# Score banks of an attention kernel taken pair by pair in the order of the exponentials, half sets written in two parts, and a new placing of the side jobs

## The reference, cut to what matters

```python
x = x + attn(layernorm(x))      # softmax(tril(q k / sqrt(8), -1)) v, then @ Wr + br
x = x + ffn(layernorm(x))
# attn
att = einsum('bhqe,bhke->bhqk', q, k) / sqrt(he)
att = softmax(att * tril(ones, k=-1))
# ffn
scores = where(causal, einsum('bqhd,bkhd->bhqk', q, k) * scale, -inf)
x1 = layer_norm(x + (softmax(scores) @ v) @ out_proj_w.T + b)
gates = softmax(x1 @ gate_w.T + gate_b); top_gates, top_idx = top_k(gates, 2)
moe_out = sum(sel_experts(x1) * top_gates)
return layer_norm(x1 + moe_out)
```

## Time and profile before

| | |
|---|---|
| median of 3 runs | 795.78 us (795.67 to 799.67) |
| the profiled execution | 796.04 us, its span 794.3 us |
| PE busy | 651.4 us (82%) |
| ACT busy | 654.6 us (82%) |
| DVE busy | 394.4 us (50%) |
| POOL busy | 321.0 us (40%) |
| exponentials (ACT, L1378) | 576, 596.5 us |
| granted TensorE clock | 0.954 on average |

### The profile page before, as it was taken

One profiled execution on the slowest core, in us unless ns is written; L12 is line 12 of the kernel. 1 busy time (PEld: TensorE's weight loads), 2 busy tenths in 40 slices (PEclk: granted clock), 3 DMA queues, 4 the chain that ended last, 5 costly groups with the idle time before them and its releaser, 6 DMA issues. The chain is left out here.

```text
span 794.3 us, 15432 instructions
## 1 busy us (share of the span) xinstructions
PE 651.4 (82%) x5560; PEld 245.9 (31%) x5560; DVE 394.4 (50%) x1089; ACT 654.6 (82%) x748; POOL 321.0 (40%) x635
## 2 busy tenths in 40 slices
PE   4588997888799889889988888888978888977753
PEld 3233332333233233233322322223322332323421
DVE  5364453346446643376455633465544522545575
ACT  1589899998798789999889999998879989895341
POOL 3252336215633325334643344435633344333244
PEclk9699999999999999999999999999999999999776
DMA  7856457644667414434545533423635243300010
GB/s 181 276 190 209 135 163 242 200 122 161 205 211 242 160 53 126 134 108 129 186 132 160 173 114 119 135 77 125 204 120 176 93 135 111 109 27 14 1 40 28
DMA packets 76993, 109.79 MB, mean 138 GB/s; under 512 B 13784, under 2 KB 28256, under 8 KB 76896
## 3 DMA queue, kind: packets, MB, share of 16 engines
q1 hardware_dynamic: 72944, 107.32, 42.8%
q10 hardware_dynamic: 3952, 1.30, 0.7%
HBM read 60.91 MB, written 47.68 MB: 137 GB/s over the span
## 5 line engine op out<-in xcount | busy, mean ns | idle before, releaser
L1378 ACT ACTIVATE probs<-scores,shift 128x1024 f32<-128x1024 f32 x576 | 596.5, 1125 | 70.0 <-PE scores L1183 64.4
L1454 POOL TENSOR_SCALAR_AFFINE_SELECT probs<-probs 128x256 f32<-128x256 f32 (+1 forms) x448 | 195.7, 453 | 366.1 <-ACT probs L1378 365.5
L1212 PE MATMUL acc<-probs,v 128*9 128x512 f32 (+3 forms) x3072 | 318.9, 503 | 4.1 <-ACT num L1300 4.1
L1183 PE MATMUL scores<-qs,ks 32*128 32x512 f32 (+3 forms) x1536 | 159.1, 428 | 74.9 <-ACT probs L1378 72.9
L1183 PEld LDWEIGHTS scores<-qs,ks 32*128 32x128 f32 x1536 | 72.4, 187 | 272.5 <-ACT probs L1378 208.2
L1212 PEld LDWEIGHTS acc<-probs,v 128*9 128x9 f32 x3072 | 58.9, 100 | 105.2 <-issue 66.7
L1501 DVE TENSOR_TENSOR prod<-side,G 128x512 f32<-128x512 f32 x41 | 28.3, 691 | 84.3 <-PE side L1165 84.2
L1165 PE MATMUL side<-we,x1T 128*128 128x512 f32 x92 | 53.0, 659 | 0.7 <-DVE part L1550 0.7
L1435 POOL TENSOR_TENSOR moe<-psum 128x256 f32<-128x256 f32 x32 | 25.0, 781 | 67.6 <-DVE psum L1501 55.3
L1300 ACT ACTIVATE num<-acc 128x512 f32<-128x512 f32 x64 | 38.6, 603 | 5.7 <-PE acc L1212 5.6
L1410 POOL TENSOR_TENSOR rstd<-rstd,expo 128x4 f32<-128x4 f32 x32 | 33.3, 1041 | 2.7
(11 more groups left out here) (193 smaller groups left out, 605.6 us busy)
## 6 DMA issues: line engine op xcount, KB each, us to landing
ks<-k_dram SPq DMA_DIRECT2D x96, 256.0 KB, 4.2
q_dram<-part SPq DMA_DIRECT2D x64, 256.0 KB, 3.2
qs<-q_dram SPq DMA_DIRECT2D x64, 256.0 KB, 3.7
num_dram<-num SPq DMA_DIRECT2D x60, 256.0 KB, 2.7
k_dram<-part SPq DMA_DIRECT2D x30, 256.0 KB, 3.6
xrow<-in_x SPq DMA_DIRECT2D x16, 256.0 KB, 4.5
nat<-num_dram SPq DMA_DIRECT2D x15, 256.0 KB
rdenb<-rden_dram SPq DMA_DIRECT2D x15, 256.0 KB
```

Of the source, the lines that this page charges most:

```text
L1183: ins = pe.matmul(scores[:, pair(g, h // 2), h % 2, col:col + w], ks[u][r, kt // TH, (kt % TH) * P:(kt % TH + 1) * P], qs[u][r, q0:q0 + w] ...
L1212: ins = pe.matmul(acc[h * VW:h * VW + VC, q0:q0 + w], v9[V_OF[k]][:, kt, :, HG * hg + h], src, start=(s == 0), stop=last, skip_group_check ...
L1378: act.activation(dst, src, ACT.Exp, bias=shift[:, column(k):column(k) + 1], scale=SCALE).then_inc(probs_raw, 1)
L1454: ins = pool.affine_select(out=blocks, in_=blocks, compare_op=ALU.is_ge, fill=0.0, base=a - 1, pattern=[[0, blocks.shape[1]], [1, P]], cha ...
```

## The change

1. **Pairs by exponential.** Unit `n` (the n-th exponential) has pair `n % 3`. A half set takes one pair: heads 0 and 1 in columns 0 to 255 of its two banks, heads 2 and 3 in columns 256 to 511 of the same banks. PE waits for the exponential three units before the set's last one. Behind a half set that is the exponential before the half set's own.
2. **A half set in two parts.** Since heads 0 and 2 (1 and 3) now share a bank, PE writes heads 0 and 1, then does the values of the set three earlier, then waits for its own first part (`half_scores`) and writes heads 2 and 3; only this tells ACT that the scores are there.
3. **The planner.** `ahead` is measured against the time at which ACT is through with what it has, less the next set's scores; `LATE` goes from 0.5 to 0.2, `UNIT_TIME` from 1.15 to 1.1; the plan's PE and ACT clocks follow points 1 and 2. The due times of `p3`'s stores move later by 50 units and more, so that `p2` stands before `p3`.
4. Slots become `STRETCHES` that could be cut in halves. They aren't here: there is one for each slot, with both halves, and `rows_half` gives the same rows as before.

The diff, cut to its core:

```diff
-def pair(g, i):
-    return (2 * g + i) % PAIRS
...
-    ends[x("store")] = at(k + 2, 40 * j)
+    ends[x("store")] = last_by(k, b, j) + 50
...
-UNIT_TIME = 1.15
-LATE = 0.5
+UNIT_TIME = 1.1
+LATE = 0.2
...
-            ahead = t + (0.49 * len(UNITS_OF[g - LAG]) if p % 2 == 0 and g >= LAG else 0.0) - exps[FIRST_UNIT[g]] - 0.1
+            ahead = t + (values(g) if p % 2 == 0 else 0.0) + next_scores(g) + 0.08 - clock["ACT"]
...
-        def half_block(g, h):
-
-            return h if pair(g, 0) < pair(g, 1) else (h + 2) % HG
+        def place_of(g, h):
+
+            units = UNITS_OF[g]
+            if len(units) == 1:
+                return units[0], h % 2, HALF // 2 * (h // 2)
+            return units[h // 2], h % 2, 0
...
-                else:
-
-                    pe.wait_ge(probs_raw, FIRST_UNIT[g - 1] + 1)
...
+                elif last >= PAIRS:
+
+                    pe.wait_ge(probs_raw, last - PAIRS + 1)
+                if is_half(qh, s):
+                    heads_scores(g, (0, 1), shifted).then_inc(half_scores, 1)
                 else:
...
+                    heads_scores(g, range(HG), shifted).then_inc(scores_ready, 1)
+
+            def other_heads(g, shifted):
+
+                pe.wait_ge(half_scores, HALVES_TO[g])
+                heads_scores(g, (2, 3), shifted).then_inc(scores_ready, 1)
...
                     if g >= LAG:
                         value_group(g - LAG)
+                    if len(UNITS_OF[g]) == 1:
+                        other_heads(g, shifted)
...
-                if len(UNITS_OF[g]) == 1:
-                    low_, high = sorted((pair(g, 0), pair(g, 1)))
-                    src = scores[:, low_:high + 1:high - low_, :, 0:HALF // 2]
-                    dst = probs[n % NPB][:, :, :].rearrange("p a (c s) -> p a c s", c=2)
...
+                src = scores[:, n % PAIRS, :, :].rearrange("p c s -> p (c s)")
+                dst = probs[n % NPB][:, :, :].rearrange("p c s -> p (c s)")
```

More of the change, by code:

```diff
@@ L1 @@
+import itertools
 from contextlib import ExitStack
@@ L36 @@
 NSLOT = len(SLOTS)
+STRETCHES = [(k, (0, 1)) for k in range(NSLOT)]
 def sets_of(qh):
@@ L149, in takes, with stretch_of, pass_of, rows_half @@
     return sum(turn_time(x)[1:])
+def stretch_of(k, qh):
+    return next(st for st, (k_, halves) in enumerate(STRETCHES) if k_ == k and qh in halves)
+def pass_of(k, i):
+    return next(gp for gp in range(NP) if PASS_OF[gp][1] == k and (PASS_OF[gp][2], PASS_OF[gp][3]) == PASSES[i])
+def rows_half(b, j):
+    order = [(SLOTS[k][1], qh) for k, halves in STRETCHES if SLOTS[k][0] for qh in halves]
+    return order[2 * b + j]
+BOUNDS = [(b, 0) for b in range(B)]
+def bound_of(k, _halves):
+    return BOUNDS.index((SLOTS[k][1], 0))
 def at(slot, unit):
-    return slot * UB + unit
+    return (STRETCH_FIRST[stretch_of(slot, 0)] if slot < NSLOT else NU + (slot - NSLOT) * UB) + unit
 def slot_of(a, b):
@@ L238, in p2 @@
         out[x("v")] = [x("xT")]
-        ends[x("parts_out")] = ends[x("v")] = at(k, -12)
+        ends[x("parts_out")] = ends[x("v")] = STRETCH_FIRST[stretch_of(k, j)] - 12
         if j:
[L241 to L245, removed]
+            n = 0
+            out[("p2", b, "top", n)] = [x("norm"), x("norm", 1)]
+            out[("p2", b, "tops", n)] = [("p2", b, "top", n)]
+            out[("p2", b, "roots", n)] = [("p2", b, "tops", n)]
+            out[("p2", b, "shift", n)] = [("p2", b, "roots", n)]
+            ends[("p2", b, "shift", n)] = STRETCH_FIRST[stretch_of(k, 0)] - 4
     def p3(b, j):
@@ L395, in finish, with exponentials, values, next_scores @@
         done[x] = begin + dve + 0.1
+    def exponentials(units):
+        for n in units:
+            clock["ACT"] = max(clock["ACT"], clock["PE"] + 0.08) + 1.0
+            exps[n] = clock["ACT"] + 0.12
+            for gp in range(NP):
+                if evacuated(gp) == n:
+                    clock["ACT"] += 0.48
+                    done[("evacuated", gp)] = clock["ACT"] + 1.5
+    def values(g):
+        return 0.49 * len(UNITS_OF[g - LAG]) if g >= LAG else 0.0
+    def next_scores(g):
+        if g + 1 == SETS_ALL:
+            return 0.0
+        return 0.44 if len(UNITS_OF[g + 1]) > 1 else 0.3 + values(g + 1)
     for p in range(NPOINT):
@@ L1250, in _, with stretch @@
             pe.wait_ge(narrowed, n_narrow)
-            def slot(k, shifted):
-                for g in range(k * GB, (k + 1) * GB):
+            def stretch(st, shifted):
+                for g in range(STRETCH_GROUP[st], STRETCH_GROUP[st + 1]):
                     scores_set(g, shifted)
```

356 lines of the change are left out of this document (196 added, 160 removed).

## The result

The changed kernel takes **804.43 us** (median of 20 runs, 798.97 to 811.78), the kernel before, run beside it on the same chip, 798.61 (20 runs, 795.23 to 804.33): a ratio of **1.0069, 95% interval 1.0046 to 1.0092**. The forecast was 758, faster by 5%. The profiled execution of the changed kernel took 798.97, with a span of 797.2 and a mean granted clock of 0.949 (before: 794.3 and 0.954). That is the fastest of its runs: the three at 0.949 took 798.97 to 801.16, the seventeen others, at 0.929 to 0.945, longer.

The account below looks back on a forecast made before the run. PE and ACT were taken to hold each other up in turn, neither full. Stretch -31 (-38 + 4 + 3 + 0) and tail -7 took 796.04 to 758 us; forecast 744 to 770, wider range 742 to 781.

Parts of the forecast that it names:

- Part 1, first half: Exponentials opening a pass: without a job behind the half set the hole closes; 29 with one keep 0.35 us each.
- Part 1, the gain of 38: 63 pass openings: holes cost 48 us today, 10 stay, so 38 us are gained (22 to 48).
- Part 2: Half sets' scores in two parts: 0.2 us more PE work each, 13 us over 64, costing +4 us (0 to 20).
- a third of it: Share of the split's 13 us of PE work that is paid, only where PE is the later engine.
- no hole: Half sets' own exponentials: scores come about 0.3 us later when PE waits for ACT, leaving ACT without a hole.
- second part comes late: Rival at half sets: exponential delayed behind values and second part, 64 x 1.05 = 67 us, 808 in total; chance 0.07.
- Part 3, +3 and 0 (-10 to +15): Planner: six more jobs before the tail cost +3 us (0 to 7); other holes in the stretch change by 0.
- The tail, -7 (0 to -12): After the last exponential: 7 of 23.6 us between `acc`'s last copy and the last half's sum are saved.
- -31: Stretch from first to last exponential: -38 + 4 + 3 + 0, from 693.1 to 662 us.

Follow-up runs that it names:

- run 1: Against the kernel before: new banks and two-part half sets with the old job table, 1.0056; old banks with the new job table, 1.0072.
- Run 3: The kernel before with only its half sets' scores split in two, the second part waiting for the first: 822.55 us, 1.0271.
- run 2: Changed kernel with the half set's second part directly behind the first, ahead of the values: 0.9971 to the kernel before; with the old job table 1.0052.
- run 5: Kernel before and changed kernel, each with values matmuls cut to three quarters of their columns: 0.9959 and 0.9947 to the kernel before.

## Why the prediction was wrong, point by point

**Part 1, first half: right.** "With no job in between, the hole closes": 34 such openings hold 0.0 us. With a job behind the half set 0.35 each was forecast, and 29 of them hold 6.3, 0.22 each. The holes before openings fell to 6.3 us, where "about 10" was forecast.

**Part 1, the gain of 38: the step that failed.** The sum of the holes was read rightly, their evenness not: of the 63, only some 30 hold about 0.7 us and more with nothing in them, and 22 hold 0.20 to 0.22, where ACT copies `acc` in the gap. What failed is how they were priced. It took 41.0 us of idle at openings as time that the change frees. A hole that closes is a gain only if the next thing that ACT needs is there in time. Of the 63 openings 42 had a job ahead, and at 27 of these PE was late by its own work and waited for no exponential (26.0 of the 41.0 us); 15.0 us at the 36 others stood behind the bank's exponential. The earlier trace rows were read as PE's own hole, and still counted as gain wherever the new order put the job elsewhere. The job's 1 us of PE is not gone by that: it meets the half set instead. PE idled 98 of 693 us before and 87 of 703 after. Openings lost 34.7 us of holes, half sets took back 38.4 (4.3 to 42.7), and the other places gained 6.6; the sum, +10.3, is what the stretch grew by.

**Part 2: the work was sized right; "a third of it" paid and "no hole" failed.** I took 0.2 us of PE for the extra group, 13 us over 64. At full clock the second part takes 0.31 us where a job follows (390.44 to 390.75 above). Where the next scores follow without a wait, they start 0.01 us behind it, on the two strips that it leaves free, and both together take 0.11 us more than the scores alone (0.55 us in 12 such places, as from 411.71 to 412.26, against 0.44, as from 414.31 to 414.75). 29 x 0.31 + 35 x 0.11 is 13 us; with the old table's 42 jobs it is 15, and PE's busy time rose by 15.9 there (run 1). The 25.1 us by which the busy time of these groups rose count the time that they share with the next scores. So the argument that the next scores can start under the second part held, and 0.114 us was its price; that the columns alone set the time did not hold where a job follows.

What failed is what comes of it. Run 3 puts a split that waits for its first part at some 22 us, most of its 28 us of PE paid; how much of the 13 us is paid in the changed kernel no run separates, since the second part's place goes with it. And "half sets' scores are there 0.3 us later: no hole" holds only for the 42 half sets without a job ahead, 0.24 us each; of the 22 with one, 21 held about 1.1 each and one 9.4. The place behind the values was priced at nothing but this; with the new table it costs 1.0% (run 2).

The rule cited there (TensorEngine Tiling (Array Packing), Key Properties, of the Trainium skill) tells of drains at a change of mode. The trace fits it as far as it goes: 0.11 us where scores follow scores, 0.31 us where another kind of matmul follows. That a drain is the reason for the difference, no run here shows.

**The rival "second part comes late": its mechanism is what happened.** It gave 1.05 us for each late half set, and ones with a job ahead cost that. But it put all 64 at that price (67 us, 808 in total), and only the third with a job ahead paid it. That 804 lies near its 808 is luck: it also counted 48 us won, where the openings gave 34.7. I gave it 0.07, on the ground that PE waited at half sets before. That wait was PE's slack under the old banks; with the new banks it is down to 0.3 us. That the parts and the six jobs more are what spent it is argued, not shown.

**Part 3, +3 and 0 (-10 to +15).** The new table alone costs the stretch 11.4 us with the old banks, inside the bounds and far from the centre. One late input makes 9.4 of the holes of the kernel after. The prediction had such inputs as its upper end, in chains through POOL and DMA; the large one ran through DVE's stop at a slot's opening, which it had not seen.

**The tail, -7 (0 to -12): right,** -7.5, and in each kernel with a new table -6.4 to -8.6. The place was half right. From `acc`'s last copy to the last half's sum it is now 17.4 us and not 23.6, but the copy itself comes 2.2 us later behind the last exponential; so the sum begins 21.2 us after the last exponential, 25.2 before. The other 3.5 us were won behind the sum, which the prediction had not counted:

```profile
734.49 0.60 ACT L1398 ACTIVATE num<-acc 128x512 f32<-128x512 f32 x1 [3.82 <-PE scores L1170]
...
751.85 0.68 DVE L1596 TENSOR_TENSOR xrow<-scores,xr 128x512 f32<-128x512 f32 x1
```

**Sum.** Forecast -31 and -7; measured in the profiled executions +10.4 and -7.5, which is 2.9, and a further 3 in the medians. Its median run has a lower clock than its profiled one (0.941 against 0.949); why the clock fell, no run tells by itself.

## What to carry to other kernels

When two engines hold each other up in turn, sort the idle time before a given step by whether its releaser was waiting itself. Only that part belongs to the wait that a change removes; the other is the releaser's own work, and it comes out again at the next step that needs it. A group of side-by-side matmuls that is split has no single price: here the second half cost 0.31 us of PE, as much as the whole group, ahead of other work, 0.11 ahead of matmuls that could start beside it, and 0.44 where it had to wait for the first half. And a signal that a waiting engine needs belongs ahead of the work that it doesn't need. A change of structure should be timed with a plan made from its own traced durations: here the same structure was worth -1.5% or +0.5% by the table alone.

## What had not been expected

**Less work on PE bought a lower clock.** Cutting PE's busy time by 27 to 37 us took the granted clock in the stretch from 0.97 to 0.94 and 0.92 (run 5), and the time fell by 0.4 to 0.5% only. It is so in every execution: the mean clock of the ten and ten with the cut was 0.909 to 0.928 and 0.879 to 0.922, that of the kernel before beside them 0.941 to 0.959. The clock fell at the large hole too, as two windows of the kernel after show:

```profile
404.00:414.00 10.00, 9.52 (x72) 3.10 (x68) 5.17 (x14) 8.73 (x9) 4.58 (x10) 1.00 0.51 157
464.00:476.00 12.00, 9.13 (x62) 4.30 (x66) 3.63 (x16) 3.73 (x5) 1.45 (x3) 0.50 0.19 68
```

After PE had stood still for 5.8 us the granted clock was 0.50, the level of 1.2 GHz, and two value groups in one row took 1.90 us; the same row at full clock:

```profile
414.75 1.06 PE L1307 MATMUL acc<-probs,v 128*9 128x384 f32 x16
```

So this standstill cost its own time and then made the next work dear. The Trainium skill (TensorE: Matmul & The Clock Gate, What's actually happening) says that the clock has two levels set by how busy PE has been of late; the two windows agree with that.

**DVE's stop.** It stands for 3.4 us at a slot's opening with nothing that it waits for (460.97 to 464.71 above). The same trace has one of 2.8 to 4.1 us at six of the seven later slot openings, and the kernel before has them too. What DVE does in them is open. One thing the trace does show: in this one the only DMA packet of the core is one of instructions (window 461.28 to 464.71, queue, kind, packets, MB, share):

```profile
q14 instruction: 1, 0.01, 0.6%
```

The other five have such a packet in them as well, so a stop for code behind the branch is a candidate; no run tests it. Telling the planner of the stops (0.9917 against 0.9855) didn't help.
